# Moving GpSimd's row transfers behind the next tile's scale, and reading the picked rows' numbers two experts after they are written

## The reference, cut to what matters

```python
x = x + 0.5 * ffn(layernorm(x), gate_w, gate_b, w1, w2)
x = x + attn(layernorm(x), Wq, bq, Wk, bk, Wv, bv, Wo, bo)
x = x + 0.5 * ffn(layernorm(x), gate_w, gate_b, w1, w2)

def ffn(x, gate_w, gate_b, w1, w2):
    # softmax over the tokens of a sequence; each of 32 experts takes its 8 best tokens
    vals, idx = top_k(softmax(x @ gate_w.T + gate_b, over="tokens"), 8)
    merged = sum_k(x[idx] * vals)              # one vector per sequence and expert
    h = gelu([merged, 1] @ w1[e])              # 513 x 2048
    o = [h, 1] @ w2[e]                         # 2049 x 512
    return zeros_like(x).at[idx].add(o * vals) # back to the picked tokens

def attn(x, ...):
    q, k, v = exp(heads(x @ Wq.T + bq)), exp(heads(x @ Wk.T + bk)), heads(x @ Wv.T + bv)
    num = einsum(q, cumsum(k v^T))             # causal, 16 heads of 32
    return (num / sum(q * cumsum(k))) @ Wo.T + bo
```

## Time and profile before

| | us |
|---|---|
| runs shown | 2288.2, 6017.0, 2282.41 |
| their median | 2288.2 |
| the profiled execution | 2283.05 |
| its span, first to last instruction | 2281.3 |
| first pass over the experts, about | 145 to 930 |
| attention loop, about | 950 to 1645 |
| second pass, about | 1660 to 2281 |

### The profile page before, as it was taken

One profiled execution on the slowest core, in us unless ns is written; L12 is line 12 of the kernel. 1 busy time (PEld: TensorE's weight loads), 2 busy tenths in 40 slices (PEclk: granted clock), 3 DMA queues, 4 the chain that ended last, 5 costly groups with the idle time before them and its releaser, 6 DMA issues.

```text
span 2281.3 us, 43539 instructions
## 1 busy us (share of the span) xinstructions
PE 1962.4 (86%) x18440; PEld 1161.6 (51%) x18440; DVE 728.5 (32%) x1235; ACT 779.3 (34%) x1413; POOL 622.9 (27%) x756
## 2 busy tenths in 40 slices
PE   5789999999999999889999999999776566656667
PEld 4546666666666666666777776777521111111111
DVE  6731111111111111367777677677410000000011
ACT  6831111121111111357777777677510000000000
POOL 7610000000000000267777777777412000000002
PEclk9999999999999999999999999999897867787777
DMA  9999999999999999776776676676499999999997
GB/s 366 357 398 404 418 401 428 430 426 422 427 418 429 418 423 415 219 261 212 250 262 224 229 249 214 198 258 209 184 406 425 427 399 428 428 428 428 428 427 332
DMA packets 133202, 804.49 MB, mean 353 GB/s; under 512 B 31240, under 2 KB 31368, under 8 KB 91792
## 3 DMA queue, kind: packets, MB, share of 16 engines
q1 hardware_dynamic: 116880, 713.29, 79.0%
q10 hardware_dynamic: 9216, 50.34, 5.3%
q0 software_dynamic: 6912, 38.07, 4.3%
HBM read 678.24 MB, written 136.95 MB: 357 GB/s over the span
## 4 chain that ended last, share of the span: by engine, by line
PE 59%; DMA 24%; ACT 5%; POOL 5%; issue 4%; SPq 1%; DVE 1%; POOLq 0%; DVEq 0%; ACTq 0%
PE ps L349 54%; DMA big<-in_L_ffn_w 22%; PE ps L353 3%; SPq L18 1%; DMA last_scratch<-idx 1%; ACT big L635 1%; POOL big L1599 1%; POOL s L1602 1%; ACT big L620 1%; PE ps L824 1%; POOL big L1572 1%; ACT big L625 1%; DMA row_scratch<-idx 1%; PE ps L512 0%; ACT big L1391 0%
## 5 line engine op out<-in xcount | busy, mean ns | idle before, releaser
L349 PE MATMUL ps<-big 128*32 128x512 f32 (+5 forms) x13568 | 946.7, 412 | 229.9 <-DMA big<-in_L_ffn_w 179.9
L349 PEld LDWEIGHTS ps<-big 128*32 128x32 f32 (+2 forms) x13568 | 374.1, 126 | 727.4 <-issue 383.6
L357 DVE TENSOR_TENSOR big<-ps,big 128x128 f32<-128x128 f32 (+4 forms) x277 | 266.7, 966 | 697.9 <-PE ps L824 511.6
L349 PE MATMUL ps<-wth,xth 128*128 128x512 f32 x768 | 311.8, 406 | 1.5 <-DVE xtl L357 1.5
L349 PE MATMUL ps<-wtl,xth 128*128 128x512 f32 x768 | 299.6, 390 | 0.0
L349 PE MATMUL ps<-wth,xtl 128*128 128x512 f32 x768 | 299.3, 390 | 0.0
L872 ACT COPY big<-ps 128x512 f32<-128x512 f32 x64 | 37.5, 586 | 644.1 <-PE ps L349 623.3
L1544 POOL TENSOR_SCALAR big<-big 128x1 f32<-128x1 f32 x8 | 1.5, 188 | 827.6 <-ACT ps L1351 827.2
L1024 DVE TENSOR_SCALAR big<-ps,big 128x512 f32<-128x512 f32 x64 | 48.1, 751 | 533.7 <-PE ps L349 533.7
L1015 ACT ACTIVATE big<-ps,big 128x512 f32<-128x512 f32 x128 | 88.2, 689 | 371.8 <-PE ps L349 356.1
L349 PE MATMUL ps<-wo,s 128*128 128x512 f32 x768 | 210.0, 408 | 3.0 <-ACT s L1436 1.4
(11 more groups left out here) (140 smaller groups left out, 1761.8 us busy)
## 6 DMA issues: line engine op xcount, KB each, us to landing
big<-in_L_ffn_w SPq DMA_DIRECT2D x254, 2048.0 KB, 35.9
p_weight_x_scratch<-big ACTq DMA_DIRECT2D x64, 768.0 KB, 11.2
big<-p_weight_x_scratch SPq DMA_DIRECT2D x64, 768.0 KB, 5.7
xt_scratch<-big SPq DMA_DIRECT2D x16, 1024.0 KB, 8.6
big<-xt_scratch SPq DMA_DIRECT2D x16, 1024.0 KB, 16.2
x_weight_scratch<-big SPq DMA_DIRECT2D x64, 256.0 KB, 3.2
out_x<-big SPq DMA_DIRECT2D x64, 256.0 KB, 4.0
big<-in_L_attn_x SPq DMA_DIRECT2D x15, 1024.0 KB, 11.3
```

The source lines that it names most:

```text
L349: return nc.tensor.matmul(o, l, r, start=start, stop=stop, skip_group_check=True)
L357: return nc.vector.tensor_tensor(o, p, q, op)
```

## The change

Two things are moved, and nothing is added or taken away. On SP the read of the row numbers, which stood right behind their write in expert 6, gets a function of its own and is issued in expert 8. On GpSimd the row transfers of a round go from the place between `ATL` and `qb` to the end of the round.

```diff
@@ experts_sp
                 if p == 0 and e == 6:
                     rows_sp(sp)
+                if p == 0 and e == 8:
+                    rows_read_sp(sp)
@@ attention_pool
                     nc.gpsimd.tensor_tensor(ATL, AT, ATH.bitcast(F), ALU.subtract).then_inc(s_atl, 1)
-                for i in range(2):
-                    if turn(n, i):
-                        rows_gather_pool(pool, turn(n, i), i)
-                for i in range(2):
-                    if turn(n, 5 + i):
-                        rows_scatter_pool(pool, turn(n, 5 + i), i)
                 m = n + 2
                 if m < NT:
...
                 if 8 * TILED <= n + 3 < NT:
                     pool.wait_ge(s_kl, n + 3)
                     scale_pool(n + 3)
+                for i in range(2):
+                    if turn(n, i):
+                        rows_gather_pool(pool, turn(n, i), i)
+                for i in range(2):
+                    if turn(n, 5 + i):
+                        rows_scatter_pool(pool, turn(n, 5 + i), i)
@@ rows_sp
             for h in range(2):
                 sp.dma_start(idxd[h], IDX1[:, 8 * h:8 * h + 8]).then_inc(d_row, 16)
+
+        def rows_read_sp(sp):
             sp.wait_ge(d_row, RW0 + 32)
             sp.dma_start(IDXG.rearrange("r (b i) -> r b i", i=2), ...
```

## The result

The changed kernel takes 2336.3 us (median of 6), the kernel before 2286.9 (6 executions in the same comparison, of which the one at 6017.0 us is not in the ratio): a ratio of 1.0211, with a 95% interval of 1.0192 to 1.0229. The forecast was 2309, with a range up to 2324. The profiled execution after took 2330.65 us with a span of 2328.9, against 2283.05 and 2281.3 before, so 47.6 us are to be found between the two traces, where the forecast had 25.6.

The account below looks back on a forecast made before the run. PE was taken to bound the attention loop, the weights' loads to end the second pass. 2283.05 - 1.1 (read) - 3.3 (scatters) + 20.9 (gather waits) + 9 (clock) = 2308.6, forecast 2309 us, range 2291 to 2324.

Parts of the forecast that it names:

- With the same time to its last packet: Second gathers behind the scale, 4.9 us later, duration as before: PE waits 17.3 us in all for sequences 3 to 7.
- The second rival: Gathers land sooner in the new place, at 5.6 us or a little under, no clock fall: 2294 us, chance 0.10.
- The Trainium skill's rule: A GpSimd transfer takes 2.0 us fixed plus bytes over 436 GB/s: 4.5 us per gather, sum about 2288.
- Sequence 1, put at nothing: Gathers in round -1: what `KL` wins is spent waiting for rows; nothing, between 1.3 won and 1 lost.
- sequence 2, put at 3.6 and 1.5 for the clock: Gather 6.9 us later, PE waits 4.5, of which 3.6 remain after the `qn` wait; clock fall 1.5 more.
- The clock, put at 9: PE's clock falls behind six new waits, each costing 0 to 3.0 us; the middle, 1.5, taken: 9 us.
- The reading of rows 14: The attention loop's one clock fall, 964.2 to 971.0, cost half of PE's 6.06 busy us in the following stretch: 3.0 us.
- The scatters, put at -3.3: Second scatters behind the scale let `KL` come about 1.1 us sooner; net 0.55 won per sequence, 3.3 in six.
- The read, -1.1: Row numbers read two experts later: SP does not stop and expert 7 gets back 1.1 us.
- Gathers are in time: Rival: no PE wait for gathers and the scatters' wait goes; 2278.7 us, down to 2274; chance 0.08.
- The filled cover: Idle time ahead of `x2ve`, 1.24 us, just covers a 1.3 us transfer; if gone, 18 transfers cost `qn` up to 23 us.
- the last rival: All six clock falls at 3.0 us and `qn` late by 1.3 in 18 rounds: 2344; chance over 2% slower 0.08.

Follow-up runs that it names:

- Run 3: The changed kernel with SP issuing nothing more, in rounds where PE takes rows of sequences 2 to 7, until the second gather has landed: 2318.7 us, 1.0144.
- run 4: The changed kernel with 16 matmuls of 128x512, whose results nobody reads, ahead of PE's wait for the gathers: 2321.4 us, 1.0162.
- run 5: The kernel before with the read moved and the scatters of sequences 2 to 7 at the end of their rounds, all gathers in place: 2282.5 us, 0.9989.
- run 8: The kernel before with only the read of the row numbers moved behind expert 7's loads: 2282.8 us, 0.9988.

## Why the prediction was wrong

The mechanism was right: PE waits for the second gather, once per sequence, and nothing behind it gives the time back. The sum was too small by 22 us, in its sizes. By the two traces sequences 1 and 2 cost 17.4 us where 5.1 stood, sequences 3 to 7 cost 35.1 where 24.8 stood (17.3 and five times 1.5), the other rounds gave 2.3 where the scatters were to bring 3.3, and up to round 0 and behind the loop 2.6 us were won where the read was to bring 1.1.

- **"With the same time to its last packet"** is the step that failed. It took a gather's time over from the old place. By the counter the second gathers of sequences 2 to 7 took 5.9 to 7.4 us there. In the new place SP issues the round's loads and stores, one of 768 KB among them, 0.5 to 3.5 us behind the gather (sequence 4), and these gathers take 7.6 to 9.7. For sequences 3 to 7 the term was 17.3 and measured 25.0: the gathers are 6.1 us longer in sum, and 2.0 more pass between the last packet and the counter in the old place (0.4 a gather), which the prediction put at nothing. Run 3 gives 15.7 with most of that traffic held back; its five gathers were 3.2 us shorter in sum than in the old place, which more than made up for those 2.0. The second rival asked whether the new place meets other transfers, but only in the direction of sooner. The Trainium skill's rule named there (DMA: Bandwidth & Descriptors, "Anatomy of one DMA — SWDGE (gpsimd) path") came out still further off: an estimate of 4.5 us, against 5.8 to 7.1 with SP held.
- **Sequence 1, put at nothing,** cost 8.3 us, and sequence 2, put at 3.6 and 1.5 for the clock, 9.1. For sequence 1 the same step failed: the issue came at 965.82, close to the 966.2 worked out, but the gather took 10.24 us instead of 7.40 by the counter. In the trace 1.32 MB of SP's queue run beside it, where the old place had none; no run took them away for this sequence, so here the cause is argued. PE took the rows at 976.20 and not 973.37, and the fall lasted 10.2 us instead of 6.8. For sequence 2 the issue moved 7.2 us against `ATL` (6.9 worked out), and the gather took 9.69 instead of 5.91.
- **The clock, put at 9,** was priced for six falls, and seven came. The reading of rows 14 holds: half of the time that PE is busy inside the falls is 15.5 us (30.95, above), 2.2 for each, and run 4, which left one fall, won 14.9 (11 by the ratios). Less the 3.0 of the fall that was there before, 12.5 stand against 9. Sequences 3 to 7 lost 10.1 beyond the waits (35.1 less 25.0) where 7.5 stood. Neither the middle, 1.5, nor the bound, 3.0, was the size.
- **The scatters, put at -3.3,** brought 0.6 in rounds 8 to 56 of run 5 and nothing that the medians tell, in the changed kernel at most the 2.3 of the other rounds. The waits for `KL` went as described and `qn` got part of them; missing was DVE, which by the reading of run 5 meets GpSimd more often at their common port.
- **The read, -1.1,** was right: expert 7 takes 26.2 us without a wait, and the interval of run 8 (0.9979 to 0.9997) holds the forecast near its upper end.
- "Gathers are in time" fell with the first row of the waits. The filled cover gave way only in part: waits for `qn` are 1.9 us in all and not 23, and the last rival's 2344 was near the time for another reason than its own.

The versions that beat both kernels leave the gathers in their old place: the read alone (0.9988) or with the scatters of sequences 2 to 7 (0.9989).

## What to carry to other kernels

When a transfer is moved in a list, its duration does not move with it: look up which queues issue in the new place within its time, and price it with that traffic beside it. A transfer whose result is needed in the same round has only the slack that the trace shows, here 0.6 to 2.1 us, and every microsecond past it stops PE, which here also lost clock behind each of the seven waits. Before a stall of one engine is removed, look at what its silence may be good for: a shared port (argued here from the overlaps), or a transfer that had time to land.

## What the runs showed of the hardware

- An indirect gather of 1.07 MB in 144 packets took 5.98 us with 0.07 MB of SP's traffic beside it, 7.25 us with 1.02 MB and 8.23 us with 1.25 MB. The other way round, SP's two stores of 256 KB in that round land 6.7 and 7.7 us after their issue beside the gather, and 3.3 and 4.1 us where they are issued 5.6 and 6.0 us behind it.
- The granted clock was at its lower level for 3.4, 6.8 or 10.2 us around and behind waits of 4.3 to 9.7 us. The same 16 matmuls took 1.08 us there and 0.62 us at the upper level.
- An operation of DVE on SBUF that starts behind one of GpSimd takes up to 1.80 us instead of 0.69, and GpSimd's takes 1.72 instead of 1.29 when DVE is first.
